# Graph network kernel: GpSimd makes half of the basis products of the first convolution

## What is computed

```python
def spline_basis(pseudo):                      # pseudo: [E, 3]
    pos = pseudo * (KS - 1)                    # KS = 5
    i0 = jnp.clip(jnp.floor(pos), 0, KS - 2).astype(jnp.int32)
    frac = pos - i0
    basis = jnp.prod(jnp.where(combos[None] == 1, frac[:, None, :], 1.0 - frac[:, None, :]), axis=-1)
    idx = jnp.sum((i0[:, None, :] + combos[None]) * strides[None, None, :], axis=-1)
    return basis, idx
...
h = jnp.ones((N, 1), x.dtype)
h = jax.nn.elu(spline_conv(h, row, col, basis, idx, stn1_w, stn1_b))
```

## Time and profile before

| what | us |
|---|---|
| median of 3 runs | 11165.09 |
| lowest and highest of them | 11158.27, 11210.48 |
| span of the profiled execution | 12528.6 |
| the first convolution in it, from its first to its last DVE instruction | 3259.17 to 3989.27 |

### The profile page before, as it was taken

How to read it: one execution, slowest core, us unless ns; L and a number is a source line. 1 busy time by engine, 2 the same in 40 slices (tenths; PEclk the granted TensorE clock), 3 DMA queues, 4 the chain that set the end, 5 groups by cost and what they waited for, 6 DMA issues and landing times. The chain is left out here.

```text
span 12528.6 us, 178083 instructions
## 1 busy us (share of the span) xinstructions
PE 6505.4 (52%) x38968; PEld 5397.9 (43%) x38968; DVE 7716.2 (62%) x17239; ACT 2933.1 (23%) x8407; POOL 7476.5 (60%) x7456
## 2 busy tenths in 40 slices
PE   3466666666475799999994444545555100000000
PEld 2355555555475677777764434434454100000000
DVE  9844444444498676666664444544576267777777
ACT  0011111111132344344432222322343000000001
POOL 5155555655200888888886888888800566666663
PEclk9966666666698999999997667766777555555555
DMA  1210000000733444444443333333322212221221
GB/s 41 65 36 2 2 2 2 2 2 2 14 41 50 93 93 94 92 94 95 92 93 49 50 51 53 54 50 52 54 42 34 35 49 50 51 50 48 51 54 40
DMA packets 1788557, 605.09 MB, mean 48 GB/s; under 512 B 1595943, under 2 KB 1729575, under 8 KB 1788260
## 3 DMA queue, kind: packets, MB, share of 16 engines
q1 hardware_dynamic: 1078132, 311.05, 12.8%
q0 software_dynamic: 255648, 274.30, 10.7%
q10 hardware_dynamic: 454736, 19.28, 3.0%
HBM read 430.75 MB, written 172.95 MB: 48 GB/s over the span
## 5 line engine op out<-in xcount | busy, mean ns | idle before, releaser
L1222 PE MATMUL c_acc<-c_spread_sb,c_basis_sb 128*125 128x256 f32 (+1 forms) x12544 | 2599.2, 376 | 1502.8 <-issue 655.0
L1222 PEld LDWEIGHTS c_acc<-c_spread_sb,c_basis_sb 128*125 128x125 f32 x12544 | 2266.5, 231 | 1803.5 <-issue 1536.3
L1614 POOL DMA_INDIRECT at_ring<-gat_table,at_place x1568 | 1585.7, 1011 | 1188.5 <-issue 1188.5
L609 POOL DMA_INDIRECT rec<-rk_rec,rk_place x1568 | 1619.3, 1033 | 1110.1 <-DVE rk_place L497 620.7
L1321 ACT ACTIVATE c_sums<-c_acc 125x512 f32<-125x512 f32 (+1 forms) x3136 | 1489.3, 490 | 2258.7 <-PE c_acc L1222 1298.6
L961 POOL DMA_INDIRECT c_ring<-hid_table,c_at x1568 | 1707.1, 1089 | 478.9 <-issue 443.2
L961 POOL DMA_INDIRECT c_ring<-feat_table,c_at x1568 | 1602.7, 1022 | 478.1 <-issue 462.9
L1084 DVE TENSOR_TENSOR c_spread_sb<-c_mark,c_rin 128x512 f32<-128x512 f32 (+1 forms) x3136 | 1745.2, 557 | 60.3
L1871 PE MATMUL gr_hps<-ident,gr_hs 128*32 128x128 f32 x98 | 29.8, 408 | 2473.7 <-issue 2066.3
L492 DVE CUSTOM_DVE_ANT_0 rk_junk_l<-rk_look_ps,rk_hi 128x98 bf16<-128x98 f32 x1568 | 402.2, 257 | 1324.1 <-remote 821.1
L1234 PE MATMUL c_mix<-c_sums,c_w 125*64 125x256 f32 (+1 forms) x9408 | 1037.3, 401 | 187.6 <-issue 133.8
(11 more groups left out here) (356 smaller groups left out, 10126.9 us busy)
## 6 DMA issues: line engine op xcount, KB each, us to landing
c_rin<-rows SPq DMA_DIRECT2D x3136, 42.0 KB
c_rin<-rows SPq DMA_DIRECT2D x3136, 20.0 KB
rows<-c_ring POOLq DMA_DIRECT2D x392, 128.0 KB
rows<-rk_blank SPq DMA_DIRECT2D x112, 252.0 KB
rows<-c_ring POOLq DMA_DIRECT2D x392, 72.0 KB
rows<-at_ring SPq DMA_DIRECT2D x196, 144.0 KB
rec<-rk_rec,rk_place POOLq DMA_INDIRECT x1568
c_ring<-hid_table,c_at POOLq DMA_INDIRECT x1568
```

The lines of the kernel that those rows point to most:

```text
L609: pool.indirect_dma_start(out=d.rec, out_offset=bass.IndirectOffsetOnAxis(ap=place[:, u, j:j + 1], axis=0), in_=rec[:, u, j, :], in_offset ...
L1222: last = pe.matmul(acc[pp % BANKS][:, (w % 2) * WN * feats:(w % 2 + 1) * WN * feats], basis[:, q, w, :, :].rearrange("p a b -> p (a b)"), ...
L1614: pool.indirect_dma_start(out=ring[:, u, j, :], out_offset=None, in_=d.gat_table, in_offset=bass.IndirectOffsetOnAxis(ap=place[:, u, j:j + ...
```

## The change

POOL gets a program in this phase: for each block it waits for `plane`, makes the second half of `basis` from the same operands, and counts it in a semaphore of its own. DVE makes the first half only, and signals ahead of it that `plane` is done. PE waits before tile 9 for POOL's semaphore in place of DVE's second count.

```diff
+    plane_made, late_made = sem("c1_plane_made"), sem("c1_late_made")
...
                 make_mark(half)
                 after_step(2)
+                dve.sem_inc(plane_made, 1)
                 make_basis(0)
-                make_basis(half)
                 dve.wait_ge(mark_made, item * 2 + 2)
                 dve.sem_inc(seq, 1)
...
+        @block.gpsimd
+        def _(pool):
+            def body(b, item, r, use):
+                u, w = r % 2, slice(half, BT)
+
+                pool.wait_ge(plane_made, item + 1)
+                pool.tensor_tensor(basis[:, u, w, :, :],
+                                   bc(plane[:, u, w, :, :].rearrange("p t a b -> p t (a b)").unsqueeze(3),
+                                      [P, half, 25, 5]),
+                                   bc(hat[:, r, w, 2, :].unsqueeze(2), [P, half, 25, 5]), ALU.mult).then_inc(late_made, 1)
+            ahead_loop(pool, c.block_passes[:, 0:1], body)
...
                     if t % half == 0:
                         pe.wait_ge(mark_made, item * 2 + t // half + 1)
-                        pe.wait_ge(basis_made, item * 2 + t // half + 1)
+                        pe.wait_ge(late_made if t else basis_made, item + 1)
```

## The result

The changed kernel takes 11237.3 us in the median of 4 runs (11234.71 to 11238.65), the kernel before 11161.7 us in the same comparison (11155.82 to 11210.48). The ratio of the times is 1.0059 with a 95% interval of 1.0038 to 1.0081: slower by 75.6 us, a small change, but one that the interval keeps clear of none.

What follows compares the result with a forecast made beforehand. DVE alone bounds the first convolution: 6.276 us per block, less 1.24 for the removed product, plus 2.5 and 0.05 for POOL, is 7.59; +1.31 times 94 blocks is +123, so 11165 becomes 11288 us. Own range 11248 to 11339, stated 11150 to 11455.

Steps and rivals of the forecast that it cites:

- rival B: First convolution: engines take turns, but POOL's turn is only 1.09 us; -9 us, 11156 us, no change; chance 0.13.
- 94 blocks count: First convolution: blocks 4 to 97 run at DVE's pace, 6.276 us each, so the per-block difference counts 94 times.
- the first four do not: Early stall of DVE behind ACT: gives the first four blocks slack, so they were costed at nothing.
- the end moves along: Phase end: DVE's 6.87 us wait for the last store of `keep` follows the last block and moves with it.
- The two engines take turns: First convolution: POOL's product fits only between two DVE instructions and DVE waits for it; +1.31 us per block, chance 0.62.
- The turn: POOL's product of 1125 numbers, holding DVE up once per block: taken as 2.5 us, between 2.07 and 3.04.
- handing over: Between the end of a DVE instruction and POOL's end, read from POOL's copies: 0.05 us per block.
- The lower row bound: POOL's product with its two inputs read one after the other: 2.07 us, giving +83 us in total.
- The copy's price per number: POOL's copy of 16 numbers, scaled: 5 ns per number, so 5.75 us for the product as the far end.
- A: First convolution: POOL's product runs under DVE's instructions, DVE's 5.04 us set the pace; -117 us, 11048 us; chance 0.12.
- C: First convolution: POOL's product is much slower, 5.75 us per turn; +429 us, 11594 us; chance 0.07.
- D: First convolution: PE, idling more, drops to its lower clock and becomes the bound at 9.35 us per block; +289 us, 11454 us; chance 0.06.

Runs made afterwards that it cites:

- run 1: Changed kernel, with DVE also waiting by semaphore for POOL's product before making its own half of `basis`: `rel` every 7.19 us, 11258.6 us in one run.
- run 2: Changed kernel, but DVE makes both halves of `basis` and POOL's product goes additionally into an unread tile: `rel` every 8.252 us, 11376.8 us.
- run 4: Changed kernel, but DVE makes both halves of `basis` and POOL only zero-fills 1125 numbers of an unread tile: `rel` every 6.278 us, 11176.1 us.
- run 5: Changed kernel with the ramp, one of `mark`'s two inputs, read from PSUM: 11128.8 us in the median, ratio to the kernel before 0.9972.
- run 8: Changed kernel with both marks moved behind `plane` and the ramp in PSUM: 11122.1 us, ratio to the kernel before 0.9962.
- run 7: Changed kernel with both marks moved behind `plane`, the ramp still in SBUF: `rel` every 6.89 us, 11209.5 us in one run.

## Why the prediction was right

The sign and the mechanism held; the size was too large. The measured 11237.3 us lie below the forecast's own range, 11248 to 11339, and inside the stated one, 11150 to 11455, only because that was drawn down to take in rival B at 11156. At 0.59% slower it is barely over the 0.5% at which the prediction drew the line to no change.

**DVE is the bound, 94 blocks count, the first four do not, the end moves along.** All held: 59.42 of 60 us, the early stall of 84.49 us, and +71 us from 94 blocks against +70.6 for the phase and 75.6 for the total.

**The two engines take turns.** This was read from POOL's copies of 16 numbers, which showed POOL waiting for DVE only. That DVE waits for POOL's whole instruction in the same way was taken over by symmetry, and is now shown by the 3.30 us of `basis` and by runs 1 and 2. The place was right too: POOL stands waiting under the second `mark` and goes first. The Trainium skill (SBUF — State Buffer, section "Who interferes with whom") says the same, and that the conflict is with GpSimd's reads and not its writes; run 4 agrees, 6.278 us beside a memset. It also says that a VectorE instruction with at most one SBUF input, outside the modes that use two ports, has no conflict; run 5 agrees, POOL's product of 2.18 us beside a `mark` that keeps its 1.35.

**The size was off, in one term.** The turn was put at 2.5 us and 0.05 for handing over, 2.55; it is 1.98. The lower row bound, "with the inputs one after the other, 2.07", was nearly the answer, and going halfway from there to 3.04 was the error: run 4 shows that the output costs DVE nothing, and POOL's 2.18 us from start to end in run 5, far under 3.04, leave no room for a third stream behind the two reads. With 1.98 the sum gives (1.98 - 1.24) x 94 = +70 us, 11235 us. The copy's price per number, 5 ns, was nearly all start-up, as suspected: 1125 numbers of one input held DVE for 0.92 us, not for 5.6. The estimate from the Trainium skill (GPSIMD Engine Reference, section 3.1), 2.47 us, was also too long; measured are 2.03 us behind `mark`, or 2.18 from start to end when nothing is in its way.

**The rivals.** A, side by side, did not come, and run 2 excludes it for instructions of this kind; it is what happens under `mark` once that has one input in SBUF (run 5). B put the turn at 1.09 us and needed one under 1.8; it is 1.98, which is why the result lies so near to no change, and the sign was right by a small margin. C did not come. Of D one part did: blocks of PE longer than 5 us rose from 16 to 35 of 94, but, as argued, 5.83 us fit under 7.02. The text forecast about 3 us of PE's wait for `basis` per block; it is 166.0 us in all, 1.8 us per block (127.2 before), because a block lasts 7.02 us and not 7.59, and PE's 18 tiles take 4.81 us in the mean where they took 4.45:

```profile
PE c_acc L812 <- DVE c_basis_sb L748: 166.0, 90, 2.9
```

**The span of the profile.** The text ahead of the prediction took the 12% for the profiler's doing. It was not: the changed kernel's profiled execution has a span of 11234.8 us at a time of 11236.7. Carrying the difference over unscaled was right for another reason, that this phase was not part of the excess.

## What to carry to other kernels

Moving a product of two SBUF inputs from DVE to POOL lost time here, because DVE's loop is made of instructions with two inputs in SBUF: the price is POOL's reading time, about 0.9 us per 1000 numbers and input, 1.98 us for this product, against the 1.24 us that DVE saved. An offload that reads one input held DVE for 0.92 us; whether that would pay depends on what DVE saves, and was not tried. Look in the trace for any POOL instruction that ran under such a DVE instruction, however small, and compare its end with the end of the DVE instruction. The ways out that these runs show are to give DVE something to do meanwhile that reads one operand from PSUM (runs 5 and 8), or to give POOL work that only writes (run 4); and then to ask which chain is next. Here it was the stores: landing and issue together take 5.86 us per block in run 8, only 0.4 us under the old 6.28.

## What was not expected

- An instruction of DVE that POOL holds up is not shown as waiting: it is shown as running, 3.30 us for work of 1.32, and the list of waits has no row in which DVE waits for POOL. Only the duration against the same form elsewhere tells.
- Reading one of two `tensor_tensor` inputs from PSUM cost VectorE nothing: 1.351 us against 1.355 for 1152 numbers.
- Moving the marks behind `plane` gained 0.13 us per block by itself (6.89 against 7.02 us). The rows show 0.11 of it: in the changed kernel `mark`, which needs `rel`, begins 2999.43 - 2999.17 = 0.26 us after it, and in run 7 the hats, which do not need it, begin 3001.29 - 3001.14 = 0.15 us after it.
